# GpSimd forms a sixth of each long part of the weights and finishes the rows in a graph-attention kernel's second stage

## The chip, the cores and the metric

One core of a Trainium2 chip. The metric is the time of one execution on the device, in microseconds. The engines are called as the profile calls them: PE (TensorE), DVE (VectorE), ACT (ScalarE), POOL (GpSimd) and SP (SyncE, which issues DMAs here).

## What is computed

x is [4096, 128] in f32, adj a [4096, 4096] matrix of zeros and ones (about 16 ones in a row), W [128, 128], a [256, 1]. Two layers, cut to their core:

```python
# first layer: for each node the maximum over its neighbours, then a layer norm
out = where(has_nbr, max over neighbours of x, 0)
x = layernorm(x + out)
# second layer: attention over the neighbours
h = x @ W
e = leaky_relu((h @ a_src)[:, None] + (h @ a_dst)[None, :], negative_slope=0.2)
att = softmax(where(valid, e, -1e9), axis=1)            # valid: adj > 0 and h.sum(1) != 0
attention = where(att >= 1e-4, att, 0) * L[:, None]     # L: number of valid neighbours
x = layernorm(x + elu(h + attention @ h))
```

## The kernel before, in words

The 32 tiles of 128 rows are worked on in 8 groups of 4 tiles, the 4096 sources in 32 segments of 128. Each engine has a queue of its own, written out by hand, and the engines meet at semaphores.

**First stage** (to about 620 us). For each group PE turns the adjacency (L1017), ACT writes it out as fp8, and PE, ACT and DVE select the first neighbour of each segment and keep maxima (L1447, one input in PSUM, one in SBUF). POOL clears the gather buffer G (memsets, L687 and L692) and issues the indirect DMAs for further neighbours (L699, L708). These go on for the last groups until about 708 us, beside the start of the second stage. Behind them POOL has nothing to do until `ex_listed`, near the end.

**Second stage.** The attention weights of a group (512 rows) against a segment are one tile [128 sources, 512 rows]. With rho a row factor and r_col a column factor, a weight is (1 + max(rho * r - 1, 0)) * adjacency. `PARTS` cuts the 32 segments into four long parts of 6 segments and two of 4. `ORDER` lists the 48 parts of all groups; from position 23 on the groups 4 to 7 follow nearly one after the other: (4, 0..2) are 23 to 25, (3, 5) is 26, (4, 3..5) 27 to 29, group 5 is 30 to 35, group 6 is 36 to 41, group 7 is 42 to 47. `BEGUN` is 4. For step i of the queues:

- ACT, `relu_part(i)` and `relu_segs` (L843 to L870): one activation of 128x512 for each segment, max(r * rho - 1, 0), into `wbuf[i % 4]`. It waits until PE has used the buffer (`w_used`, four parts earlier). ACT also has exp, log and square root of the finished groups (L906 to L914), each with a table load.
- DVE, `mask_piece(i, n)` (L1688): (w + 1) * adjacency, one instruction for a part from step 14 on (in pieces of two segments ahead of it). It reads two SBUF tensors, and it waits for the loaded adjacency and for `relu_ready`.
- PE, `weigh(i)` (L1217): 4 f32 matmuls a segment, sums in PSUM.

`ENDS` gives the step at which DVE takes the finished sums of each group (23, 26, 29, 32, 35, 38, 43, 49), and `NORM` the step of its last work on it (27, 30, 33, 36, 39, 42, 47, 52). On DVE a group g goes through: `take_sums` at ENDS[g] (L1753): small instructions, four that form u from PSUM (L1773), then e4 = min(u, 0) and p4 = max(u, 0); ACT then takes exp of e4 (`uexp`). `elu_norm` at ENDS[g] + 1 (L1797): y4 = e4 - 1 + p4 (L1802), y4 += x1in (L1805, after which SP may load x1in again, `x1_used`), statistics (L1808, L1811), variance. `find_suspects` follows (L1784). At NORM[g] come `finish` (L1815): reciprocal (L1817) and four instructions of 128x128 that write out4 (L1822), then `place_suspects` (L1826 to L1841), on whose last instruction PE waits in `list_suspects` (L1255, at its step ENDS[g] + 3). For group 7 all this stands at the end, behind the last part. SP stores a group's rows at its step ENDS[g] + 7.

The tail behind 898 us (group 7's rows, then up to 128 suspect rows computed again exactly, then a flag) follows PE's last part.

## Time and profile before

| | |
|---|---|
| runs (3) | 943.18, 944.92, 947.7 us, median 944.92 |
| profiled execution | 951.18 us |
| its span, first to last instruction | 949.4 us |
| busy of the span: PE, DVE, ACT, POOL | 725.3, 586.1, 585.2, 329.9 us |
| mean granted clock of TensorE | 0.847 |

The runs agree within half a per cent. The profiled execution is one more, 0.7% above their median; every duration here comes from it. "Busy" of PE is modelled, so a busy PE is not one at its peak; spans on POOL are rough. In a view of instructions in order of time a row has start, duration, engine, line, operation, out<-in with shapes, and a count of merged instructions; instructions of DVE overlap by some 0.08 us where nothing is waited for, so that start to start is what counts. In square brackets stands the idle time ahead of a row and who ended it.

### The profile page before, as it was taken

The page shows a single profiled execution, that of the slowest core. Times are in us where ns is not written, and L with a number is a line of the kernel's source. Part 1 is how long each engine was busy: PE and PEld are TensorE (multiplying, and loading weights), DVE is VectorE, ACT ScalarE, POOL GpSimd, SP SyncE. Part 2 cuts the span into 40 slices and gives each one's busy share as a digit, 9 for nine tenths or more (in the row PEclk, how much of TensorE's full clock was granted, in tenths as well). Part 3 has the DMA queues.
Part 4 walks back from the last instruction along what each step waited for, and adds up shares of the span by engine and source line. Part 5 has one row for each costly group of instructions (what it writes and reads, how often), then busy time and mean ns, then how long its engine had stood idle before and what let it go on. Part 6 is the DMA issues. An engine that isn't in the chain of part 4 may idle for free.

```text
span 949.4 us, 17279 instructions
## 1 busy us (share of the span) xinstructions
PE 725.3 (76%) x6605; PEld 529.3 (56%) x6675; DVE 586.1 (62%) x1319; ACT 585.2 (62%) x861; POOL 329.9 (35%) x310
## 2 busy tenths in 40 slices
PE   4999469659677946955966783688999798999843
PEld 2566236325334523632633441387999698999832
DVE  4668129337525724833752662499957699999673
ACT  5998248328425724822842653578785799999570
POOL 4101751761462374176157136406860000000020
PEclk9999669668957957976986795789999999999957
DMA  9977436444364434744536121222413123232030
GB/s 187 210 152 157 76 73 134 96 90 103 85 123 88 110 72 82 156 85 88 101 94 129 40 71 27 89 77 80 123 38 101 56 87 87 73 109 59 12 59 2
DMA packets 60512, 87.37 MB, mean 92 GB/s; under 512 B 7714, under 2 KB 33326, under 8 KB 60428
## 3 DMA queue, kind: packets, MB, share of 16 engines
q0 software_dynamic: 27328, 42.14, 26.2%
q1 hardware_dynamic: 33100, 44.10, 14.8%
q8 instruction: 55, 0.90, 0.4%
q14 instruction: 29, 0.24, 0.1%
HBM read 108.12 MB, written 21.04 MB: 136 GB/s over the span
## 4 chain that ended last, share of the span: by engine, by line
PE 35%; DVE 19%; another core or an unknown queue 19%; ACT 10%; issue 10%; POOL 5%; DMA 0%; POOLq 0%; DVEq 0%; ACTq 0%
PE psS L1046 13%; PE psA L1017 5%; PE psR L1027 5%; PE psR L1236 3%; DVE x_split L1694 3%; POOL G L699 3%; DVE acc L1447 3%; DVE adj_in L1694 3%; ACT hot L784 2%; ACT at_home L777 2%; PE psC L1061 2%; PE psC L1065 2%; ACT adj_in L865 1%; ACT x_split L865 1%
## 5 line engine op out<-in xcount | busy, mean ns | idle before, releaser
L1447 DVE TENSOR_TENSOR acc<-acc,psS 128x1024 f32<-128x1024 f32 x120 | 146.2, 1218 | 246.9 <-remote 161.2
L1046 PE MATMUL psS<-hot,x_split 128*128 128x512 bf16 x698 | 217.5, 418 | 51.3 <-issue 41.3
L784 ACT ACTIVATE hot<-psR,is_none 128x512 bf16<-128x512 f32 x256 | 168.6, 703 | 105.4 <-remote 71.9
L699 POOL DMA_INDIRECT G<-in_x_dram,idx x160 | 178.1, 1113 | 124.8 <-DVE idx L1537 78.5
L777 ACT ACTIVATE at_home<-psA 128x1024 fp8e4<-128x1024 bf16 x128 | 133.3, 1041 | 125.1 <-remote 89.9
L1046 PEld LDWEIGHTS psS<-hot,x_split 128*128 128x128 bf16 x768 | 77.3, 103 | 127.4 <-issue 65.9
L1017 PE MATMUL psA<-ident_bf,adj_in 128*128 128x128 bf16 x1024 | 93.5, 234 | 58.7 <-issue 31.4
L1027 PE MATMUL psR<-at_home,first 128*128 128x512 fp8e4 x256 | 106.4, 416 | 12.3 <-issue 8.7
L1017 PEld LDWEIGHTS psA<-ident_bf,adj_in 128*128 128x128 bf16 x1024 | 67.5, 104 | 73.8 <-issue 45.1
L1061 PEld LDWEIGHTS psC<-taken_book,hot 128*128 128x128 bf16 x1024 | 64.1, 100 | 75.9 <-issue 29.8
L708 POOL DMA_INDIRECT G<-in_x_dram,idx_extra x80 | 84.4, 1055 | 39.7 <-issue 22.6
L1694 DVE SCALAR_TENSOR_TENSOR x_split<-x_split,at_home 128x1024 f32<-128x1024 f32 (+2 forms) x36 | 72.7, 2049 | 11.9 <-ACT x_split L865 11.8
L1065 PE MATMUL psC<-codebook,at_home 128*128 128x13 bf16 x1024 | 65.0, 169 | 15.0 <-issue 15.0
L643 POOL DMA_DIRECT2D adj_in<-in_adj_dram x28 | 22.2, 794 | 152.7 <-PE psA L1017 135.7
L1694 DVE SCALAR_TENSOR_TENSOR adj_in<-adj_in,at_home 128x1024 f32<-128x1024 f32 (+2 forms) x40 | 73.2, 1860 | 1.9 <-ACT adj_in L865 1.9
L730 POOL DMA_INDIRECT adj_in<-in_adj_dram,exact_idx x4 | 3.9, 966 | 200.2 <-DVE exact_idx L1936 199.3
L1061 PE MATMUL psC<-taken_book,hot 128*128 128x13 bf16 x1024 | 66.7, 171 | 6.5 <-issue 6.1
L1236 PE MATMUL psR<-at_home,adj_in 128*128 128x130 f32 x416 | 50.4, 283 | 11.3 <-DVE adj_in L1694 11.3
L1236 PEld LDWEIGHTS psR<-at_home,adj_in 128*128 128x128 f32 x416 | 49.3, 198 | 12.5 <-issue 12.5
L865 ACT ACTIVATE x_split<-acc,minus,r_col 128x512 f32<-128x512 f32 x72 | 51.9, 801 | 6.0 <-PE psC L1236 6.0
L1065 PEld LDWEIGHTS psC<-codebook,at_home 128*128 128x128 fp8e4 x1024 | 45.4, 97 | 15.9 <-issue 15.9
L865 ACT ACTIVATE adj_in<-rho,minus,r_col 128x512 f32<-128x512 f32 x72 | 52.2, 803 | 3.3 <-PE psC L1236 3.2
(321 smaller groups left out, 1242.4 us busy)
## 6 DMA issues: line engine op xcount, KB each, us to landing
adj_in<-in_adj_dram POOLq DMA_DIRECT2D x28, 1024.0 KB, 10.8
adjT_dram<-at_home SPq DMA_DIRECT2D x32, 512.0 KB, 7.6
at_home<-adjT_dram SPq DMA_DIRECT2D x32, 384.0 KB
adj_in<-in_adj_dram POOLq DMA_DIRECT2D x8, 512.0 KB, 8.5
at_home<-adjT_dram SPq DMA_DIRECT2D x16, 256.0 KB
G<-in_x_dram,idx POOLq DMA_INDIRECT x160
own<-in_x_dram SPq DMA_DIRECT2D x8, 256.0 KB
x_dram<-x1w SPq DMA_DIRECT2D x8, 256.0 KB
```

The costliest lines, as they stand in the source:

```text
L699: pool.indirect_dma_start(out=G[:, k * GT + t, :], out_offset=None, in_=x, in_offset=bass.IndirectOffsetOnAxis(ap=idx[:, t, k:k + 1], axis=0),
L777: nc.scalar.copy(at[:, 2 * u:2 * u + 2, :], turn_home, saturate=True).then_inc(at_ready, 1)
L784: nc.scalar.activation(hot[:, n % 4, :], psR[:, n % 2, :], ACT.Relu, bias=is_none[:, :]).then_inc(hot_ready, 1)
L865: nc.scalar.activation(home[:, s - s0, :], rho[g % 4], ACT.Relu, bias=minus1[:, :], scale=r_col[:, s:s + 1]).then_inc(relu_ready, 1)
L1017: mm = nc.tensor.transpose(turn_home[:, i, t * P:(t + 1) * P], adj_in[:, k, t, at_col:at_col + SEG], ident_bf[:, :])
L1027: nc.tensor.matmul(psR[:, n % 2, :], first[:, :], at[:, n % SEGS, :], start=True, stop=True).then_inc(ranked, 1)
L1046: mm = nc.tensor.matmul(psS[:, b, s % 2 * ROWS:(s % 2 + 1) * ROWS], x_split[:, k, s, :], hot[:, n % 4, :], start=(k == 0), stop=(k == 2))
L1061: mm = nc.tensor.matmul(code_home[:, t, j, :], hot[:, n % 4, t * P:(t + 1) * P], taken_book[:, :], start=False, stop=False, skip_group_che ...
L1065: mm = nc.tensor.matmul(code_home[:, t, j, :], at[:, s, t * P:(t + 1) * P], codebook[:, :], start=False, stop=True, skip_group_check=True)
L1236: mm = nc.tensor.matmul(sums_of(g, t)[:, 0:D + 2], home[:, s - s0, t * P:(t + 1) * P], h_f[:, s, :], start=(s == 0 and starts(g, t)), stop ...
L1447: V.tensor_tensor(acc_flat, acc_flat, psS[:, b, :], ALU.max).then_inc(free[b], 1)
L1694: mask = V.scalar_tensor_tensor(out=home[:, s0:s1, :], in0=home[:, s0:s1, :], scalar=1.0, in1=ring[:, s0:s1, :], op0=ALU.add, op1=ALU.mult)
```

## The change

POOL gets two jobs in the second stage.

1. For each long part of groups 4 to 7 (16 parts, `BY_POOL`), POOL forms the sixth segment: max(r * rho, 1), which is the relu with its 1 already added, and DVE multiplies that segment by the adjacency in an instruction of its own. ACT forms five segments, and DVE's mask covers five.
2. For groups 0 to 6, POOL does the two additions of `elu_norm` (`add_up`, two instructions of 128x512) and the four instructions that write the rows (`normalised`, 128x128 each). p4 gets its -1 in the instruction that forms it. DVE keeps statistics, variance and reciprocal; its `elu_norm` stands one step later (ENDS[g] + 2). Group 7 is finished on DVE as before.

POOL's queue of this stage stands behind the gathers: step by step relu_one, then normalised at NORM[g] + 1, then add_up at ENDS[g] + 2.

```diff
+BY_POOL = [1 if g >= BEGUN and PARTS[k][1] - PARTS[k][0] == PART else 0 for g, k in ORDER]
+POOL_DONE = [sum(BY_POOL[:i + 1]) for i in range(len(ORDER))]
+RELUS_DONE = [done - by_pool for done, by_pool in zip(SEGS_DONE, POOL_DONE)]
...
+            def add_up(g):
+                if g:
+                    pool.wait_ge(out_ready, g)
+                pool.wait_ge(uexp_ready, g + 1)
+                pool.wait_ge(pos_ready, g + 1)
+                nc.gpsimd.tensor_tensor(y4, e4, p4, ALU.add).then_inc(pool_step, 1)
+                pool.wait_ge(pool_step, g + 1)
+                pool.wait_ge(x1_loaded[g % 2], 16 * (g // 2 + 1))
+                nc.gpsimd.tensor_tensor(y4, y4, x1in[:, g % 2, :, :], ALU.add).then_inc(x1_used, 1)
+
+            def normalised(g):
+                pool.wait_ge(rstd_ready, g + 1)
+                if g >= 2:
+                    pool.wait_ge(out_stored[g % 2], 16 * (g // 2))
+                for t in range(GT):
+                    last = nc.gpsimd.tensor_scalar(out4[:, g % 2, t, :], y4[:, t, :], mv[:, t, 0:1], rstd[:, t:t + 1],
+                                                   ALU.subtract, ALU.mult)
+                last.then_inc(out_ready, 1)
+
+
+            def relu_one(i):
+                g, k = ORDER[i]
+                pool.wait_ge(w_used, i - WEIGHTS_AHEAD + 1)
+                pool.wait_ge(rho_ready, g - BEGUN + 1)
+                nc.gpsimd.tensor_scalar(wbuf[i % WEIGHTS_AHEAD][:, PART - 1, :], rho[g % 4],
+                                        r_col[:, PARTS[k][1] - 1:PARTS[k][1]], 1.0, ALU.mult, ALU.max
+                                        ).then_inc(pool_relu_ready, 1)
+
+            for i in range(len(ORDER) + STEPS_AFTER):
+                if i < len(ORDER) and BY_POOL[i]:
+                    relu_one(i)
+                for g in range(GROUPS - 1):
+                    if i == NORM[g] + 1:
+                        normalised(g)
+                    if i == ENDS[g] + 2:
+                        add_up(g)
...
             def relu_part(i):
                 s0, s1 = PARTS[ORDER[i][1]]
-                relu_segs(i, 0, s1 - s0)
+                relu_segs(i, 0, s1 - s0 - BY_POOL[i])
...
-                dve.wait_ge(relu_ready, (SEGS_DONE[i - 1] if i else 0) + s1)
+                dve.wait_ge(relu_ready, (RELUS_DONE[i - 1] if i else 0) + s1)
                 mask = V.scalar_tensor_tensor(out=home[:, s0:s1, :], in0=home[:, s0:s1, :], scalar=1.0, in1=ring[:, s0:s1, :],
                                               op0=ALU.add, op1=ALU.mult)
+                if BY_POOL[i]:
+                    dve.wait_ge(pool_relu_ready, POOL_DONE[i])
+                    mask = V.tensor_tensor(home[:, s1:PART, :], home[:, s1:PART, :], ring[:, s1:PART, :], ALU.mult)
...
-                V.tensor_scalar(p4, u4, 0.0, None, ALU.max).then_inc(dve_step, 1)
-                own_t.n += 1
-                return own_t.n
-
-            pos_mark = {}
+                V.tensor_scalar(p4, u4, 0.0, -1.0, ALU.max, ALU.add).then_inc(pos_ready, 1)
...
             def elu_norm(g):
-                after(pos_mark[g])
+
+                if g == GROUPS - 1:
+                    dve.wait_ge(out_ready, g)
+                    dve.wait_ge(uexp_ready, g + 1)
+                    dve.wait_ge(pos_ready, g + 1)
+                    a = mark(V.tensor_tensor(y4, e4, p4, ALU.add))
+                    after(a)
+                    dve.wait_ge(x1_loaded[g % 2], 16 * (g // 2 + 1))
+                    V.tensor_tensor(y4, y4, x1in[:, g % 2, :, :], ALU.add).then_inc(x1_used, 1)
+                dve.wait_ge(x1_used, g + 1)
                 if g:
                     dve.wait_ge(out_ready, g)
-                dve.wait_ge(uexp_ready, g + 1)
-                a = mark(V.scalar_tensor_tensor(out=y4, in0=e4, scalar=-1.0, in1=p4, op0=ALU.add, op1=ALU.add))
-                after(a)
-                dve.wait_ge(x1_loaded[g % 2], 16 * (g // 2 + 1))
-                V.tensor_tensor(y4, y4, x1in[:, g % 2, :, :], ALU.add).then_inc(x1_used, 1)
-                dve.wait_ge(x1_used, g + 1)
...
             def finish(g):
                 dve.wait_ge(std1_ready, g + 1)
+                if g < GROUPS - 1:
+                    V.reciprocal(rstd[:, :], std[:, :]).then_inc(rstd_ready, 1)
+                    return
...
+                            elu_norm(g)
+                        else:
+                            find_suspects(g)
+                    if i == ENDS[g] + 2 and g < GROUPS - 1:
                         elu_norm(g)
-                        if g < GROUPS - 1:
-                            find_suspects(g)
                     if i == ENDS[g]:
-                        pos_mark[g] = take_sums(g)
+                        take_sums(g)
```

## Rows read from the trace of the kernel before

**Rows 1.** Windows: stretch, its length, busy us (and instructions) by engine, PEclk, DMA share, GB/s
```profile
757.00:812.00 55.00, 50.95 (x435) 49.63 (x436) 53.45 (x124) 53.14 (x71) 0.00 (x0) 0.97 0.28 80
812.00:867.00 55.00, 51.28 (x445) 50.36 (x443) 51.88 (x125) 54.46 (x74) 0.00 (x0) 0.97 0.31 93
867.00:898.00 31.00, 30.83 (x277) 30.62 (x277) 23.07 (x46) 18.47 (x25) 0.00 (x0) 1.00 0.11 30
```

**Rows 2.** Waits of 757 to 898 us: total, times, longest
```profile
PE psS L1259 <- DVE base L1841: 6.2, 3, 2.8
...
PE psR L1236 <- DVE G L1773: 3.5, 1, 3.5
...
DVE x_split L1694 <- ACT x_split L865: 2.8, 2, 1.6
```

**Rows 3.** Timeline of DVE: sums of group 2 and of group 4
```profile
788.79 1.13 DVE L1773 SCALAR_TENSOR_TENSOR G<-psS,h_seg 128x128 f32<-128x128 f32 x4
...
824.56 1.13 DVE L1773 SCALAR_TENSOR_TENSOR G<-psR,h_seg 128x128 f32<-128x128 f32 x4
```

**Rows 4.** Timeline of PE: the wait for group 5's suspects
```profile
866.94 1.16 PE L1259 MATMUL psS<-h_seg,C 128*128 128x134 f32 x8 [0.87 <-DVE base L1841]
```

**Rows 5.** Timeline of DVE, masks and finishing work between 845 and 855 us
```profile
845.26 3.35 DVE L1694 SCALAR_TENSOR_TENSOR x_split<-x_split,at_home 128x3072 f32<-128x3072 f32 x1
...
848.73 1.12 DVE L1822 TENSOR_SCALAR G<-G,mv,rstd 128x128 f32<-128x128 f32 x4
849.76 0.22 DVE L1830 TENSOR_SCALAR sus_at<-psS,base 128x4 f32<-128x4 f32 x1
...
850.42 0.69 DVE L1838 TENSOR_TENSOR C<-place_iota,sus_at 128x512 f32<-128x512 f32 x1
851.03 0.15 DVE L1841 TENSOR_TENSOR base<-base,psS 128x1 f32<-128x1 f32 x1
851.09 0.68 DVE L1802 SCALAR_TENSOR_TENSOR G<-G 128x512 f32<-128x512 f32 x1
...
852.54 0.87 DVE L1808 BATCH_NORM_STATS2 stats<-G 128x6 f32<-128x128 f32 x4
...
854.60 2.29 DVE L1694 SCALAR_TENSOR_TENSOR adj_in<-adj_in,at_home 128x2048 f32<-128x2048 f32 x1
```

**Rows 6.** Timeline of ACT: six relus of a long part
```profile
864.90 4.33 ACT L865 ACTIVATE adj_in<-acc,minus,r_col 128x512 f32<-128x512 f32 x6
```

**Rows 7.** Groups by form on POOL: count, busy us, mean ns, idle before
```profile
L687 POOL MEMSET G<- 128x2560 f32 x8 | 17.9, 2242 | 45.6 <-DVE gmax L1579 45.6
L692 POOL MEMSET G<- 128x1280 f32 x8 | 9.5, 1188 | 0.0
...
L667 POOL IOTA seg<- 128x320 f32 x1 | 1.2, 1170 | 0.0
```

**Rows 8.** One line's instructions (ns, least/median/greatest), and the timelines of DVE and POOL
```profile
L1492 DVE CAST key_int<-level x8: 188/191/2322, 85.2 to 637.4; 128x64 int32<-128x64 f32 x8
...
637.40 2.32 DVE L1492 CAST key_int<-level 128x64 int32<-128x64 f32 x1
...
637.44 2.23 POOL L687 MEMSET G<- 128x2560 f32 x1 [22.91 <-DVE gmax L1579]
...
L1447 DVE TENSOR_TENSOR acc<-acc,psS x120: 1202/1221/1223, 26.0 to 615.7; 128x1024 f32<-128x1024 f32 x120
```

**Rows 9.** Groups to 640 us and of 640 to 710 us; timelines of POOL and DVE
```profile
L699 POOL DMA_INDIRECT G<-in_x_dram,idx x140 | 141.4, 1010 | 111.1 <-DVE idx L1537 70.7 <-issue 40.5
...
L699 POOL DMA_INDIRECT G<-in_x_dram,idx x20 | 36.8, 1838 | 13.6 <-DVE idx L1537 7.9 <-issue 5.8
...
682.94 7.13 POOL L699 DMA_INDIRECT G<-in_x_dram,idx  x1 [0.30 <-issue]
...
699.78 3.36 DVE L1694 SCALAR_TENSOR_TENSOR x_split<-x_split,at_home 128x3072 f32<-128x3072 f32 x1 [1.51 <-ACT x_split L865]
...
700.92 3.10 POOL L708 DMA_INDIRECT G<-in_x_dram,idx_extra  x1 [0.30 <-issue]
```

More of the change, by code:

```diff
@@ L396, in build @@
         relu_ready = sem("relu_ready")
+        pool_relu_ready = sem("pool_relu_ready")
         w_ready = sem("w_ready")
@@ L428, in build @@
         neg_ready = sem("neg_ready")
+        pos_ready = sem("pos_ready")
+        pool_step = sem("pool_step")
+        rstd_ready = sem("rstd_ready")
         ex_neg_ready = sem("ex_neg_ready")
@@ L838, in spread_rho @@
                     act.wait_ge(s_spread, g - BEGUN + 1)
-                    act.wait_ge(relu_ready, SEGS_DONE[AT[g - 4, NPARTS - 1]])
+                    act.wait_ge(relu_ready, RELUS_DONE[AT[g - 4, NPARTS - 1]])
+                    if POOL_DONE[AT[g - 4, NPARTS - 1]]:
+                        act.wait_ge(pool_relu_ready, POOL_DONE[AT[g - 4, NPARTS - 1]])
                     from_ps, done = psS[:, 0, 0:ROWS], rho_ready
@@ L1683, in pieces @@
                 g, k = ORDER[i]
-                m = PARTS[k][1] - PARTS[k][0]
+                m = PARTS[k][1] - PARTS[k][0] - BY_POOL[i]
                 step = 2 if i < BY_PIECES else m
@@ L1997, in _ @@
             dve.wait_ge(ex_u_ready, 1)
+            dve.wait_ge(out_ready, GROUPS)
             V.tensor_scalar(e4[:, 0, :], u4[:, 0, :], 0.0, None, ALU.min).then_inc(ex_neg_ready, 1)
```

## The prediction

> **What bounds the kernel now.** The windows view comes first, because an average over the span mixes stages: from 757 us, when the first group of rows is taken, to 867 us, PE, DVE and ACT are all busy for over nine tenths of the time and POOL not at all [rows 1]. So any of the three could be the limit, and the waits decide. In that stretch PE waits for DVE: 3.5 us once at its head, where it waits for group 0 to be taken, and 6.2 us in three waits for the last instruction of place_suspects; DVE waits for ACT 2.8 us in two waits [rows 2]. DVE is the limit by a little. Its period shows it too: from group 2's sums to group 4's is 35.8 us for two groups, with DVE going from instruction to instruction [rows 3]. Behind 867 us it turns: the last wait of PE for DVE ends at 866.9 us, with 0.87 us [rows 4], and from there PE is busy for 30.8 of 31 us at full clock [rows 1]. So **the end of the stage is the time of place_suspects of group 5 (DVE's step 42) plus 31 us of PE work**, and behind that comes a tail that the change leaves alone but for group 7's own rows, which stay on DVE. A microsecond taken from or given to DVE ahead of step 42 counts fully; one behind it doesn't, as DVE is busy for only 23 of those 31 us [rows 1]. POOL's last work of before is the gathering, over before the stretch starts, so the cover for what POOL gets is an idle engine, and the question is what that engine shares with DVE.
>
> **What is taken away.** Ahead of step 42 six groups (0 to 5) are finished. In each DVE loses the two additions, from 851.09 to 852.54, 1.45 us, and the four instructions that write the rows, 848.73 to 849.76, 1.03 us [rows 5]. That is 2.48 us a group, 14.9 us in all. Adding -1 in the instruction that forms p4 costs nothing: it is a second scalar operation in the same pass. ACT loses one relu of each long part of groups 4 to 7. Six of them take 4.33 us with the first at 0.80, so 0.71 each [rows 6]; 13 lie at or before step 42, 9.2 us. That alone moves nothing, since ACT is not the last to arrive, but it keeps ACT from becoming the bound when DVE is relieved: ACT is idle for only 2.4 of 110 us [rows 1].
>
> **What is added on DVE.** The mask of a long part is two instructions. One of 3072 elements takes 3.35 us and one of 2048 takes 2.29 [rows 5], 0.53 us a segment; the segment that splits off costs what a 128x512 instruction with two inputs costs from start to start, 850.42 to 851.03, 0.61 us [rows 5]. So 0.08 us each, 13 times, 1.0 us. DVE's net own saving is 13.9 us. SP's queue keeps its instructions; stores of a group wait for out_ready, which now comes about a step later, and go out 7 steps behind the group's end, so they still fit.
>
> **What is added on POOL, and its price.** 13 relus ahead of step 42, and for each of six groups two additions of 128x512 and four instructions of 128x128. No elementwise instruction that reads SBUF runs on POOL in this trace, so I bound it. Below: memsets of 2560 and 1280 elements take 2.24 and 1.19 us, 0.82 ns an element and 0.14 us on top [rows 7], so 0.56 us for 512 elements and 0.25 for 128. Above: an iota of 320 elements takes 1.17 us [rows 7], 3.7 ns an element, 1.87 us for 512. A relu has one input and one output and lies near the memset: 0.6 us. An addition brings two inputs, and I take twice the input time: 1.0 us. The four of 128 elements take 0.28 each. A group is then 2.0 + 1.1 = 3.1 us, six are 18.7, 13 relus 7.8, together **26.5 us of POOL** (20.0 with the low prices; some 58 with the iota's, which I don't believe for a plain stream). The Trainium skill (GPSIMD Engine Reference, section 3.1) gives 4497 ns for a tensor_tensor of 2048 elements, so by it an addition is an estimated 1.1 us and the sum below would be 1 us more; no run here shows it.
>
> **What POOL's time does to DVE.** This decides. At 637.40 us DVE starts a CAST of 64 elements that takes 0.19 us seven times of eight; this once it takes 2.32 us and ends when a memset on POOL ends that began 0.04 us later [rows 8]. DVE stood still for a whole POOL instruction. The other way round, a gather's issue on POOL takes 1.01 us on average up to 640 us, where DVE works mostly from PSUM, and 1.84 us behind it, where the masks run [rows 9]; the one at 700.92 us takes 3.10 us because a mask runs until 703.14, and one sat through six masks, 7.13 us [rows 9]. Against this stands stage one's maximum, whose one input is in PSUM: 120 of them lie between 1202 and 1223 ns, memsets beside some of them [rows 8]. So the two engines share something that masks and SBUF-to-SBUF scalar instructions need, and that is held for whole instructions. What no row shows is a POOL instruction that reads hundreds of elements against a mask: the bounds are none of POOL's time charged to DVE and all of it. DVE's instructions that do without are mainly the four with sums from PSUM, 1.13 us [rows 3], and the statistics, 0.87 us [rows 5], with small ones some 3 us of the 15.5 a group that DVE has left. That speaks for 0.8; POOL's instructions that fall into these run free, and I take 0.75. POOL then costs DVE 19.9 us, and the sum at step 42 is -14.9 + 1.0 + 19.9 = **+6.0 us**, carried to the end. The profiled execution, 951.2 us (span 949.4), becomes 957.2; it lies 6.3 us above the median of the runs, 944.9, which I take as base: **950.9 us**. With low prices and a share of 0.6 the sum is -2; with relus at 0.8, additions at 1.3 and a share of 0.8, +12.
>
> The Trainium skill (SBUF — State Buffer, Who interferes with whom) says just this: a DVE instruction with two SBUF inputs contends with a GpSimd one that reads SBUF, a 2-port one with any, and whoever is second blocks for the whole instruction. By it the share is near 1 and the sum +13; by a reading in which only POOL waits, it is the second rival. The trace agrees for the CAST (2.32 us) and for POOL's side; for a mask behind a reading POOL instruction no run here shows it.
>
> **Rivals.** (1) *POOL never holds a mask.* For it: every mask of 1024 elements beside POOL's issues keeps its price, and only a CAST was seen held. Then DVE saves 13.9 us, but PE can't use it all: its waits of 6.2 us and the low clock of 812 to 867 us (0.97 over 55 us, 1.65 us lost) are all that goes [rows 1, 2, 4], 7.9 us. Then 937.0 us, and PE bounds. It decides once less than 0.52 of POOL's time (13.9 of 26.5) falls on DVE; this is the other side. (2) *The exchange comes out even*, share 0.4 to 0.55: within 4 us of 945. (3) *POOL comes late.* DVE's step for the statistics waits for x1_used, hence for six POOL instructions in a row that each may sit behind a mask. DVE idles there, so that POOL's time counts in full: 26.5 less 13.9, +13 us, 958 us. Queued behind that wait are the masks, and PE behind them. For it: the 7.13 us [rows 9]; against: a whole mask and place_suspects lie between rstd_ready and the wait, 5 us. That the change doesn't do what it says is excluded by the wait structure: DVE can't mask a last segment without pool_relu_ready.
>
> **Chances.** A measurement of this kernel tells about 0.5% from no change, 4.7 us. The forecast case, -2 to +12 with its middle at +6, has 0.50; rival 1 has 0.25, rival 2 0.10, rival 3 0.15. Slower by over 0.5%: 0.31 of the forecast case and 0.14 of rival 3, 0.45. Within: 0.16 + 0.03 of rival 1 + 0.08 + 0.01, 0.28. Faster: the rest, 0.27. Both signs are well filled, so the range takes in rival 1 and most of the rest: 936 to 958; the likeliest case alone is 943 to 957.
>
> **What would show it.** Masks of 2560 elements at 2.82 us in their shortest, with many at 3.4 or more and ends that agree with ends of POOL instructions; 512-element masks between 0.7 and 1.4; POOL relus of 0.6 us at best and of several us where they sit behind a mask; periods of two groups at 37 to 38 us, not 35.8; PE's waits for L1841's successor longer than 6.2 us, with more time at the low clock; place_suspects of group 5 ending near 873 us; PE without a wait behind it. Masks all at 2.82 and 0.69 and a period near 32 us would be rival 1; long waits of DVE for x1_used, rival 3. I am wrong in kind if DVE's time per group falls.

## The result, and the profile after

The change makes the kernel slower by 1%: 953.43 us (950.57 to 958.69, 4 runs) against 944.25 us (943.18 to 947.7, 4 runs) for the kernel before on the same chip, **ratio 1.0095 with a 95% interval of 1.0069 to 1.0121**. The forecast was 950.9 us on a base of 944.9, +6.0; measured is +9.2. Sign, size and range held, and the mechanism behind them mostly did not.

The profiled execution of after takes 950.57 us (span 948.7), less than the 951.18 of before: the start of the second stage moves by some microseconds from execution to execution (the first sums of group 0 come at 749.44 us here, at 756.91 in the trace of before), and the tail takes 49.0 or 50.6 us. So the traces are compared by the stretch that the prediction was about, from the first sums of group 0 to the start of the last instruction of place_suspects of group 5 (step 42). It took 109.73 us before and takes **118.09 us** after, +8.4; from there to the sums of group 7 it is 32.16 us in both.

Section 1 of after's page:

```profile
PE 725.0 (76%) x6605; PEld 530.4 (56%) x6675; DVE 578.7 (61%) x1293; ACT 573.7 (60%) x845; POOL 439.6 (46%) x368
```

The windows of after, columns as in [rows 1]:

```profile
757.00:812.00 55.00, 49.12 (x421) 47.92 (x420) 47.64 (x118) 46.47 (x61) 32.45 (x19) 0.97 0.24 74
812.00:867.00 55.00, 48.53 (x408) 47.46 (x406) 41.40 (x96) 45.54 (x63) 41.34 (x24) 0.94 0.28 89
867.00:898.00 31.00, 30.18 (x273) 30.19 (x274) 23.95 (x44) 18.28 (x24) 20.74 (x12) 1.00 0.12 35
```

POOL gains 110 us over the whole span and DVE loses 7. But in the second window DVE is busy for 41.4 us where it was for 51.9 [rows 1], ACT for 45.5 instead of 54.5 and PE for 48.5 instead of 51.3: **no engine is full any more**. Over the stretch DVE is busy for 97 of 118 us, where it was for 105 of 110. A stage in which all have slack and all are slower is bound by a chain through several of them. The waits of after, 757 to 900 us, name its links:

```profile
POOL G L751 <- DVE rstd L1868: 43.0, 7, 12.5
ACT std L962 <- DVE mv L1863: 17.8, 7, 3.5
...
PE psS L1307 <- DVE base L1894: 12.8, 5, 4.2
DVE stats L1858 <- POOL G L744: 11.8, 5, 3.1
...
DVE adj_in L1742 <- ACT adj_in L913: 4.7, 4, 1.8
DVE x_split L1742 <- ACT x_split L913: 4.3, 4, 1.7
```

DVE waits for POOL (11.8 us), ACT for DVE's variance (17.8, a wait that before doesn't have in this window), and DVE for ACT's relus. PE's wait for place_suspects is 12.8 us where it was 6.2 [rows 2]. One turn of the chain, group 4, in the timelines of DVE, POOL and ACT:

```profile
828.59 0.17 DVE L1868 RECIPROCAL rstd<-std 128x4 f32<-128x4 f32 x1
...
828.86 6.14 POOL L751 TENSOR_SCALAR G<-G,mv,rstd 128x128 f32<-128x128 f32 x4 [4.87 <-DVE rstd L1868]
...
830.99 2.83 DVE L1742 SCALAR_TENSOR_TENSOR adj_in<-adj_in,at_home 128x2560 f32<-128x2560 f32 x1 [0.21 <-ACT adj_in L913]
...
835.09 1.27 POOL L741 TENSOR_TENSOR G<-G 128x512 f32<-128x512 f32 x1
836.44 1.27 POOL L744 TENSOR_TENSOR G<-G 128x512 f32<-128x512 f32 x1
...
837.74 0.87 DVE L1858 BATCH_NORM_STATS2 stats<-G 128x6 f32<-128x128 f32 x4 [3.11 <-POOL G L744]
...
839.26 0.20 ACT L962 ACTIVATE std<-mv 128x4 f32<-128x4 f32 x1 [3.55 <-DVE mv L1863]
839.37 3.62 ACT L913 ACTIVATE x_split<-acc,minus,r_col 128x512 f32<-128x512 f32 x5
```

rstd comes at 828.8; POOL writes group 3's rows in 6.1 us (they free y4) and adds group 4's up by 837.7, 8.9 us in all. DVE has a mask and small work for 5.8 of them and stands for the other 3.1. ACT has stood since 835.7 before its square root, and its next five relus, which wait for nothing else, start only behind it. DVE's groups by form in the stretch (columns as in [rows 7]):

```profile
L1742 DVE SCALAR_TENSOR_TENSOR x_split<-x_split,at_home 128x2560 f32<-128x2560 f32 x7 | 19.8, 2822 | 1.9 <-ACT x_split L913 1.9
L1742 DVE SCALAR_TENSOR_TENSOR adj_in<-adj_in,at_home 128x2560 f32<-128x2560 f32 x6 | 16.9, 2822 | 0.2 <-ACT adj_in L913 0.2
L1742 DVE SCALAR_TENSOR_TENSOR adj_in<-adj_in,at_home 128x2048 f32<-128x2048 f32 x4 | 10.1, 2523 | 3.3 <-ACT adj_in L913 3.3
...
L1746 DVE TENSOR_TENSOR adj_in<-adj_in,at_home 128x512 f32<-128x512 f32 x6 | 5.2, 863 | 0.0
...
L1807 DVE TENSOR_SCALAR lnrho<-h_seg,cols 128x4 f32<-128x4 f32 x5 | 2.7, 537 | 0.0
```

The masks of 2560 elements keep 2.82 us without exception: 13 of them, and POOL is at work for 74 of the 110 us from 757 to 867. POOL is mostly the one held: a line's own instructions (ns, least, median, greatest) show what the same one takes free and beside masks.

```profile
L760 POOL TENSOR_SCALAR x_split<-rho,r_col x4: 1997/2000/3616, 741.2 to 781.4; 128x512 f32<-128x512 f32 x4
L741 POOL TENSOR_TENSOR G<-G x7: 1267/1273/3360, 751.9 to 879.3; 128x512 f32<-128x512 f32 x7
L751 POOL TENSOR_SCALAR G<-G,mv,rstd x28: 789/802/3700, 771.4 to 894.6; 128x128 f32<-128x128 f32 x28
```

But a mask can be held too. One of 2048 elements, which had waited for ACT, begins 0.2 us behind an addition of POOL and takes 3.22 us for 2.29; the second addition then sits under it (timelines of DVE and POOL):

```profile
775.05 3.22 DVE L1742 SCALAR_TENSOR_TENSOR adj_in<-adj_in,at_home 128x2048 f32<-128x2048 f32 x1 [1.77 <-ACT adj_in L913]
...
774.85 1.27 POOL L741 TENSOR_TENSOR G<-G 128x512 f32<-128x512 f32 x1
776.20 3.20 POOL L744 TENSOR_TENSOR G<-G 128x512 f32<-128x512 f32 x1
```

### The profile page after: what moved, and what is told of

The parts are those of the page before. It is cut to its first block, busy times and chain, and to the rows that moved or that the text cites. A ratio compares the mean times of both kernels' runs of the same rounds, so it can differ in the third digit from the quotient of the medians.

```text
span 948.7 us, 17319 instructions
## 1 busy us (share of the span) xinstructions
PE 725.0 (76%) x6605; PEld 530.4 (56%) x6675; DVE 578.7 (61%) x1293; ACT 573.7 (60%) x845; POOL 439.6 (46%) x368
## 3 DMA queue, kind: packets, MB, share of 16 engines
q1 hardware_dynamic: 33100, 44.10, 14.4%
## 4 chain that ended last, share of the span: by engine, by line
PE 36%; another core or an unknown queue 18%; issue 13%; POOL 11%; DVE 11%; ACT 9%; DMA 0%; POOLq 0%; ACTq 0%; DVEq 0%
PE psS L1094 14%; PE psA L1065 5%; PE psR L1075 4%; PE psR L1284 3%; POOL G L707 3%; DVE acc L1495 3%; POOL G L751 2%; ACT hot L830 2%; ACT at_home L823 2%; PE psC L1109 2%; PE psC L1113 2%; POOL x_split L760 2%; POOL G L741 1%; POOL adj_in L760 1%
## 5 line engine op out<-in xcount | busy, mean ns | idle before, releaser
L716 POOL DMA_INDIRECT G<-in_x_dram,idx_extra x80 | 86.6, 1082 | 39.1 <-issue 22.6
L1742 DVE SCALAR_TENSOR_TENSOR x_split<-x_split,at_home 128x1024 f32<-128x1024 f32 (+3 forms) x36 | 68.5, 1933 | 12.6 <-ACT x_split L913 12.6
L1742 DVE SCALAR_TENSOR_TENSOR adj_in<-adj_in,at_home 128x1024 f32<-128x1024 f32 (+2 forms) x40 | 70.5, 1791 | 6.6 <-ACT adj_in L913 6.6
L913 ACT ACTIVATE x_split<-acc,minus,r_col 128x512 f32<-128x512 f32 x68 | 49.0, 800 | 6.0 <-PE psC L1284 6.0
L751 POOL TENSOR_SCALAR G<-G,mv,rstd 128x128 f32<-128x128 f32 x28 | 32.0, 1154 | 43.0 <-DVE rstd L1868 43.0
L913 ACT ACTIVATE adj_in<-rho,minus,r_col 128x512 f32<-128x512 f32 x68 | 49.3, 801 | 3.3 <-PE psC L1284 3.2
## 6 DMA issues: line engine op xcount, KB each, us to landing
adj_in<-in_adj_dram POOLq DMA_DIRECT2D x28, 1024.0 KB, 10.5
```

Source lines behind the costliest of these rows:

```text
L913: nc.scalar.activation(home[:, s - s0, :], rho[g % 4], ACT.Relu, bias=minus1[:, :], scale=r_col[:, s:s + 1]).then_inc(relu_ready, 1)
L1742: mask = V.scalar_tensor_tensor(out=home[:, s0:s1, :], in0=home[:, s0:s1, :], scalar=1.0, in1=ring[:, s0:s1, :], op0=ALU.add, op1=ALU.mult)
```

## Theories and the yardstick

The 8.4 us can be put together from after's own trace: -14.9 + 1.0 of DVE's work, 11.8 of waiting for POOL, 5.3 more of waiting for ACT (6.9 in the stretch, 1.6 before), and 5.2 by which DVE's own instructions grew (each form's mean over its mean before, times its count). That is +8.4, but a sum doesn't say what would go away with what. Three theories: **held**, the forecast's, that POOL's instructions stop DVE's; **late**, rival 3, that DVE waits for POOL's result; and **order**, which the prediction didn't have: `elu_norm` stands a step later, so ACT, whose square root keeps its place at NORM - 1, stands in front of its relus.

Two runs measure the yardstick. The kernel before takes 762 to 763 us on three of the chips used and 944 to 945 on two, so every ratio is to before on the same chip.

before_again, no edit:

> The kernel before once more, as a measure of the yardstick itself. The experiments' stretches, from the first sums of group 0 to the last instruction of place_suspects of group 5, are all set against the one trace of before, which has 109.7 us, and some of them ran on a chip whose whole time is 762 us and not 945. If the stretch is a property of the kernel alone, this run has 109.7 us within 1 us and periods of two groups at 35.6 to 35.8 us, whatever its whole time, and the ratio is 1.000 within 0.3%. If the stretch differs by 2 us or more on another chip, then the differences of 3 us and less between experiments (relus_only, norm_only, norm_relus) can't be read from it, and only the ratios stand.

Measured: 762.71 us, ratio 1.0008 [0.9980, 1.0036]; stretch 109.70 us and the same periods, with the whole run 188 us shorter: the first sums come at 570.5 us for 756.9, and the mean granted clock is 0.956 for 0.847. So the stretch belongs to the kernel and not to the chip, within 0.1 us.

after_again, no edit to after:

> The changed kernel once more, as the control for the others of this chip. All theories: 8 to 10 us above the kernel before, the stretch from the first taking of sums to place_suspects of group 5 at 118 us against 110.

Measured: 954.29 against 945.08 us, 1.0109 [1.0081, 1.0136]; stretch 118.14 us. The result repeats, and together with before_again it makes a tenth of a microsecond in the stretch readable, and 3 us in a ratio.

All stretches and ratios together (DVE's waits in the stretch, us):

| kernel | stretch, us | against before | DVE waits for POOL | for ACT | ratio to before [95%] |
|---|---|---|---|---|---|
| before | 109.7 | | 0 | 1.6 | 1 |
| after | 118.1 | +8.4 | 11.8 | 6.9 | 1.0095 [1.0069, 1.0121] |
| beside | 120.2 | +10.5 | 0 | 0 | 1.0162 [1.0093, 1.0231] |
| beside_memset | 124.1 | +14.4 | 0 | 0.5 | 1.0183 [1.0153, 1.0213] |
| relus_only | 112.8 | +3.1 | 0 | 0.5 | 1.0064 [1.0035, 1.0093] |
| rows_only | 116.7 | +7.0 | 4.8 | 12.8 | 1.0167 [1.0105, 1.0228] |
| late_sqrt | 117.1 | +7.4 | 13.2 | 4.9 | 1.0131 [1.0069, 1.0194] |
| stats_later | 117.7 | +8.0 | 0 | 9.3 | 1.0126 [1.0085, 1.0166] |
| add_first | 110.1 | +0.3 | 0 | 1.7 | 1.0009 [0.9984, 1.0034] |
| norm_only | 108.4 | -1.4 | 0 | 6.3 | 1.0004 [0.9983, 1.0025] |
| norm_relus | 107.4 | -2.3 | 0 | 1.6 | 0.9972 [0.9945, 0.9998] |
| norm_half | 105.0 | -4.8 | 0 | 1.6 | **0.9925 [0.9898, 0.9951]** |

## How much does POOL hold DVE?

**beside.** The kernel before, with after's POOL work done on a tile nobody reads; it starts where after's would, and nobody waits for it.

```diff
+            for i in range(len(ORDER) + STEPS_AFTER):
+                if i < len(ORDER) and ORDER[i][0] >= BEGUN and ORDER[i][1] < 4:
+                    pool.wait_ge(w_used, i - WEIGHTS_AHEAD + 1)
+                    beside(side[:, 1, :], side[:, 0, :], 1.0, 1.0, ALU.mult, ALU.max, op=nc.gpsimd.tensor_scalar)
+                for g in range(GROUPS - 1):
+                    if i == NORM[g] + 1:
+                        pool.wait_ge(std1_ready, g + 1)
+                        for t in range(GT):
+                            beside(side[:, 1, t * P:(t + 1) * P], side[:, 0, t * P:(t + 1) * P], 1.0, 1.0, ALU.mult, ALU.max,
+                                   op=nc.gpsimd.tensor_scalar)
+                    if i == ENDS[g] + 2:
+                        pool.wait_ge(uexp_ready, g + 1)
+                        for k in range(2):
+                            beside(side[:, 1, :], side[:, 0, :], side[:, 0, :], ALU.add, op=nc.gpsimd.tensor_tensor)
```

> The kernel before, with POOL doing instructions of the change's kinds and sizes at the same steps on a scratch tile of its own that nobody reads (16 scalar instructions of 128x512, and for each of seven groups two additions of 128x512 and four scalar instructions of 128x128). Nobody waits for POOL; the only way to lose time is that DVE is held. Held theory (my forecast, with the prices now seen: 2.0, 1.27 and 0.80 us, 60 us of POOL ahead of DVE's step 42, three quarters on DVE): 985 us or more. POOL-late theory (POOL sits behind masks, a mask never sits behind POOL, only small scalar instructions do): 944 to 948 us.

Measured: +10.5 us of stretch, 774.69 us against 762.60. That is neither of the two expectations, and lies nearer the second. DVE's groups by form in the stretch:

```profile
L1719 DVE SCALAR_TENSOR_TENSOR adj_in<-adj_in,at_home 128x3072 f32<-128x3072 f32 x6 | 20.1, 3352 | 0.0
L1847 DVE TENSOR_SCALAR G<-G,mv,rstd 128x128 f32<-128x128 f32 x24 | 11.3, 545 | 0.2
...
L1827 DVE SCALAR_TENSOR_TENSOR G<-G 128x512 f32<-128x512 f32 x6 | 6.0, 995 | 0.0
```

The row instructions go from 344 to 545 ns (4.8 us in all), the additions and the comparison that places the suspects (L1863) grow by a third each, and the masks keep 3.35 but for one, which takes 3.76. All growth is 12.5 us, against some 60 us that POOL's instructions would take unheld (13 x 2.0 + 12 x 1.27 + 24 x 0.80 = 60.4, with the least times above; this run's own are a little shorter, 1.92, 1.04 and 0.64): a share of 0.2. Which instructions are hit depends on what stands ahead of them:

```profile
630.20 3.35 DVE L1719 SCALAR_TENSOR_TENSOR adj_in<-adj_in,at_home 128x3072 f32<-128x3072 f32 x1
...
633.67 2.49 DVE L1847 TENSOR_SCALAR G<-G,mv,rstd 128x128 f32<-128x128 f32 x4
...
630.79 4.77 POOL L734 TENSOR_TENSOR side<-side 128x512 f32<-128x512 f32 x2 [1.48 <-ACT G L935]
```

POOL's additions arrive at 630.79 under a mask and come through only behind it, where they stop the four row instructions, 2.49 us for 1.12.

**beside_memset.** The same with POOL only writing: memsets of 2048, 1344 and 768 elements in the places of relus, additions and row instructions.

```diff
-                    beside(side[:, 1, :], side[:, 0, :], 1.0, 1.0, ALU.mult, ALU.max, op=nc.gpsimd.tensor_scalar)
+                    beside(side[:, 0:4, :], 1.0, op=nc.gpsimd.memset)
...
-                            beside(side[:, 1, t * P:(t + 1) * P], side[:, 0, t * P:(t + 1) * P], 1.0, 1.0, ALU.mult, ALU.max,
-                                   op=nc.gpsimd.tensor_scalar)
+                            beside(side[:, 0:2, 0:384], 1.0, op=nc.gpsimd.memset)
...
-                            beside(side[:, 1, :], side[:, 0, :], side[:, 0, :], ALU.add, op=nc.gpsimd.tensor_tensor)
+                            beside(side[:, 0:3, 0:448], 1.0, op=nc.gpsimd.memset)
```

> The side run once more with memsets of about the same lengths (2048, 1344 and 768 elements: 1.8, 1.2 and 0.8 us) in place of the instructions that read, so that POOL only writes. If what is held is the second read of SBUF, masks and two-input instructions pass and the stretch is 110 to 113 us (scalar instructions from SBUF to SBUF may still be held, as the CAST was); POOL's memsets keep their own length beside masks. If any POOL instruction holds and is held alike: 120 us as in the side run.

Measured: +14.4 us, more than either expectation had. The line of the row instructions (ns, least, median, greatest):

```profile
L1846 DVE TENSOR_SCALAR G<-G,mv,rstd x32: 329/346/1984, 774.7 to 919.1; 128x128 f32<-128x128 f32 x32
```

One turn in DVE's timeline:

```profile
832.09 3.34 DVE L1718 SCALAR_TENSOR_TENSOR adj_in<-adj_in,at_home 128x3072 f32<-128x3072 f32 x1
...
835.56 3.58 DVE L1846 TENSOR_SCALAR G<-G,mv,rstd 128x128 f32<-128x128 f32 x4
```

The long memsets as a group in the stretch:

```profile
L734 POOL MEMSET side<- 128x2048 f32 x13 | 23.6, 1818 | 30.4 <-PE psC L1260 10.7 <-PE psS L1260 9.6 <-PE psR L1260 9.5
```

And POOL's timeline beside that turn of DVE's:

```profile
832.65 6.34 POOL L734 MEMSET side<- 128x1344 f32 x4 [1.09 <-ACT G L934]
```

A memset runs beside a mask and neither notices: 1.82 us for 2048 elements, which is [rows 7]'s 0.82 ns an element and 0.14 us, and no mask over 3.36 us. The additions and L1862, with two inputs in SBUF, keep 0.69 us as well. What is stopped are scalar instructions from SBUF to SBUF: the row instructions in three of the six groups, and small ones of 4 elements. Durations count such a stop twice, since the instruction queued behind the stopped one has begun too; from start to start the row instructions lose 6.4 us and the small ones most of the other 9. So there are two pairings: **a POOL instruction that reads gets in the way of a two-input DVE one and the other way round; scalar SBUF-to-SBUF ones on DVE are stopped by a POOL instruction that only writes as well.** The Trainium skill (SBUF — State Buffer, Who interferes with whom) has just these two cases, and both runs agree with it. It also says that whoever issues first goes first and the other blocks for the whole instruction. The addition and the 2048-element mask of after, above, agree. A relu of POOL doesn't: in relus_only one of 1.99 us begins 0.12 us ahead of a mask at 578.33 us, and the mask takes 3.25 us for 2.82, so that the two run side by side for most of the relu. How often each engine comes second, which decided the price here, has to be read from the trace.

## The parts of the change

**relus_only.** POOL's relus and the split masks alone; groups are finished on DVE at their old step.

```diff
-            def add_up(g):
...
-            def normalised(g):
...
-            for i in range(len(ORDER) + STEPS_AFTER):
-                if i < len(ORDER) and BY_POOL[i]:
+            for i in range(len(ORDER)):
+                if BY_POOL[i]:
                     relu_one(i)
```

> The kernel before with the sixth segment of the 16 long parts on POOL, rows finished on DVE as before. Held theory: 13 relus of 2.0 us ahead of step 42, three quarters on DVE, and 1 us for the split masks: 965 us. POOL-late theory: a relu on POOL (2 us, with a mask ahead of it 4.7) fits beside five on ACT (3.6 us) or is late by about 1 us; DVE stays the bound and its own work grows by 0.08 us a part: 945 to 949 us.

Measured: +3.1 us, ratio 1.0064 [1.0035, 1.0093], as the second expectation had it. The split masks cost 1.0, DVE's instructions grow by 3.4, and 1.1 of waiting for ACT goes, +3.3 together. DVE is the bound here and ACT isn't, so relieving ACT alone buys only that wait.

**rows_only.** After with `BY_POOL` all 0: additions and rows on POOL, all relus on ACT.

```diff
-BY_POOL = [1 if g >= BEGUN and PARTS[k][1] - PARTS[k][0] == PART else 0 for g, k in ORDER]
+BY_POOL = [0 for g, k in ORDER]
```

> The change without the relus on POOL: additions and row-writing of groups 0 to 6 on POOL, statistics a step later. Held theory: 34 us of POOL for six groups, three quarters on DVE, less 14.9: 955 us. POOL-late theory: the chain from the reciprocal over six POOL instructions to the statistics stays, so most of the loss stays: 948 to 954 us. If the relus make the chain late, it is gone without them and the kernel is below before: 938 to 942 us.

Measured: +7.0 us, ratio 1.0167 [1.0105, 1.0228]; the loss stays, and is not gone without the relus. By its trace -14.9 + 5.7 of growth + 4.8 for POOL + 11.2 more for ACT = +6.8. Without relus in its queue POOL is less late (4.8 for 11.8). But ACT has all its relus again and still stands 8.4 us for the variance, and DVE waits for it nearly twice as long (12.8 for 6.9). Of 19 masks five are held here, by 0.17 to 1.09 us, each behind a wait of DVE for ACT in which POOL's additions began. The two parts sum to +10.1, more than the change's 8.4: it seems that POOL's relus give ACT back part of what the later step takes from it.

## Late, or order?

**late_sqrt.** After with ACT's square root of groups 0 to 6 one step later, to match.

```diff
-                    if i == NORM[g] - 1:
+                    if i == NORM[g] - (g == GROUPS - 1):
```

> The change with ACT's square root of groups 0 to 6 one step later in ACT's queue (NORM[g] in place of NORM[g] - 1), behind the relus of that step. Theory that ACT's standing still for the variance (17.8 us in all against none before) is what delays the relus: DVE's 9.0 us of waits for ACT fall to about 3 and the time falls by 4 to 6 us, to 947 to 949 us. Theory that the chain over POOL bounds the period whatever ACT does: within 2 us of the change, 951 to 955 us.

Measured: +7.4 us, 1 us better than after by the stretch; the ratio, 1.0131 [1.0069, 1.0194], can't tell it from after. ACT's wait for the variance is gone and stands at its next instruction instead (waits of late_sqrt, in the stretch):

```profile
ACT G L958 <- DVE G L1828: 18.2, 6, 4.6
DVE stats L1858 <- POOL G L744: 13.2, 5, 3.1
```

Its next instruction is the exponential, which waits for DVE's sums. DVE is the one that is behind, and moving ACT's place in the queue doesn't bring it forward. The same move in stats_later, where POOL is idle, was not run.

**stats_later.** The kernel before with nothing but the order changed: `elu_norm` one step later, all of it on DVE, POOL idle.

```diff
                     if i == ENDS[g] + 1:
...
-                        elu_norm(g)
-                        if g < GROUPS - 1:
+                            elu_norm(g)
+                        else:
                             find_suspects(g)
+                    if i == ENDS[g] + 2 and g < GROUPS - 1:
+                        elu_norm(g)
```

> The kernel before with nothing on POOL and only the change's order on DVE: additions and statistics of groups 0 to 6 one step later. Theory that the later step alone makes ACT stand still for the variance and the relus late: 3 to 5 us slower, stretch 113 to 115 us. Theory that this order costs nothing unless POOL is late: the stretch stays at 110 us within 1, the kernel within 2 us of before.

Measured: **+8.0 us, ratio 1.0126 [1.0085, 1.0166], as much as the whole change**, with not one instruction moved to another engine, and more than the 3 to 5 us expected. Its waits in the stretch:

```profile
PE psS L1259 <- DVE base L1841: 10.5, 4, 4.4
ACT std L914 <- DVE mv L1813: 8.3, 6, 2.2
DVE adj_in L1694 <- ACT adj_in L865: 5.4, 4, 2.4
DVE x_split L1694 <- ACT x_split L865: 3.9, 3, 2.4
```

And one turn in ACT's timeline:

```profile
631.27 5.74 ACT L865 ACTIVATE x_split<-rho,minus,r_col 128x512 f32<-128x512 f32 x8
637.02 1.28 ACT L914 ACT_TABLE_LOAD   x1
639.67 0.21 ACT L914 ACTIVATE std<-mv 128x4 f32<-128x4 f32 x1 [1.36 <-DVE mv L1813]
639.78 4.33 ACT L865 ACTIVATE adj_in<-acc,minus,r_col 128x512 f32<-128x512 f32 x6
```

ACT stands 8.3 us in six waits, and DVE's wait for ACT grows from 1.6 to 9.3, 7.7 us, which is the loss. ACT was busy for 53.1 and 54.5 of 55 us [rows 1], so a microsecond in which it stands for DVE comes back to DVE as a late relu.

**add_first.** After with y4, mv and rstd doubled, so that POOL adds group g + 1 up ahead of writing group g's rows. DVE's statistics no longer stand behind six POOL instructions; the later step stays.

```diff
+        y4s = [y4, y[:, :, :]]
+        mvs, rstds = [mv, sb("mv_odd", [P, GT, 2])], [rstd, sb("rstd_odd", [P, GT])]
...
-                if g:
-                    pool.wait_ge(out_ready, g)
+                if g > 1:
+                    pool.wait_ge(out_ready, g - 1)
...
-                    if i == NORM[g] + 1:
-                        normalised(g)
                     if i == ENDS[g] + 2:
                         add_up(g)
+                for g in range(GROUPS - 1):
+                    if i == NORM[g] + 1:
+                        normalised(g)
```

> The change with y4, mean and reciprocal held twice (groups take turns), so that POOL can do the additions of group g + 1 ahead of writing the rows of group g; POOL's amount of work is the same. Theory that the chain rstd, six POOL instructions, statistics costs the time: DVE's 11.8 us of waits for POOL fall below 3 and the stretch falls from 118 to 107 to 111 us, the kernel to 2 us below or at the kernel before. Theory that it is the amount of POOL's work that holds DVE: no change against the change, 118 us.

Measured: +0.3 us, ratio 1.0009 [0.9984, 1.0034]; DVE waits for nobody but 1.7 us for ACT. Taking rival 3's wait out gains 8.0 us. The expectation that blamed the chain holds, though 11.8 us of waits gone bring only 8.0. By the difference, DVE's instructions now grow by 14.1 us (-13.9 + 0.1 + 14.1 = +0.3), nearly three times after's 5.2. DVE's groups in the stretch show where:

```profile
L1749 DVE TENSOR_TENSOR adj_in<-adj_in,at_home 128x512 f32<-128x512 f32 x6 | 7.3, 1222 | 0.0
...
L1890 DVE SCALAR_TENSOR_TENSOR sus_at<-sus_at,suspect 128x4 f32<-128x4 f32 x6 | 4.8, 794 | 0.2
```

The twelve split masks take 1.22 us for 0.685 (6.4 us in all) and L1890, four elements wide, 0.79 for 0.16. While DVE stood waiting, POOL ran free; now that it doesn't stand, the two meet. Part of what looked like a wait for a result was time that POOL needs from DVE in either form. That fits stats_later too: the later step cost 8.0 us there, presumably because ACT was full, and here, with 12 relus fewer on ACT, DVE's wait for it is down to 1.7.

## What can be kept

**norm_only.** After with `BY_POOL` all 0, y4, mv and rstd doubled as in add_first, and both additions and `elu_norm` back on DVE at ENDS + 1. POOL only writes the rows, and nobody on the path waits for them.

```diff
-                    if i == ENDS[g] + 2:
-                        add_up(g)
...
+                            elu_norm(g)
                         else:
                             find_suspects(g)
-                    if i == ENDS[g] + 2 and g < GROUPS - 1:
-                        elu_norm(g)
```

> Only the row-writing of groups 0 to 6 on POOL (with y4, mean and reciprocal held twice), additions back on DVE at their old step, no relus on POOL. DVE saves 6.2 us ahead of step 42 and nobody waits for POOL. If POOL holds DVE as in the side run (a fifth of its 19 us, about 4 us), the stretch is 107 to 109 us and the kernel 1 to 3 us faster than before. Held theory with three quarters: 8 us slower.

Measured: -1.4 us of stretch, as expected, but ratio 1.0004 [0.9983, 1.0025], where 1 to 3 us less were expected; behind the stretch it loses 1.7 us again (below). DVE is relieved of six times 1.03 us, its instructions grow by only 0.3, and 4.7 of the 6.2 come back as waits for ACT (6.3 for 1.6): ACT is now the bound.

**norm_relus** and **norm_half.** norm_only with POOL's relus for all 16 long parts, or for 8 (the first and the fourth of each group).

```diff
-BY_POOL = [0 for g, k in ORDER]
+BY_POOL = [1 if g >= BEGUN and k in (0, 3) else 0 for g, k in ORDER]
```

> norm_only with all 16 sixth segments on POOL, which is the change without its two additions and with the doubled buffers. POOL has about 13 x 2.0 + 24 x 0.8 = 45 us of work in 110 us. Cheap-POOL theory: ACT relieved by 9.2 us, DVE -6.2 + 1.0 + 3.4 of holds as in relus_only: stretch 107 to 108.5 us, the kernel 1 to 3 us below before. Theory that the relus wait behind the row-writing (3.2 us and masks): DVE waits for them and the stretch is 110 us or more.

> norm_only with the sixth segment of 8 of the 16 long parts (the first and the fourth of each group) on POOL as well. In norm_only ACT had become the bound: DVE waited 12.2 us for it ahead of step 42. Theory that POOL's work is cheap as long as nobody waits for a chain over it: ACT is relieved by 0.71 us in each of 7 parts ahead of step 42, DVE gets 0.6 us of splits and about 1.5 us of holds; the stretch falls from 108.3 to 105 to 107 us and the kernel to 2 to 5 us below before. Theory that any relu on POOL costs as in relus_only (3 us for 13): 110 us, no gain.

Measured: norm_relus -2.3 us and 0.9972 [0.9945, 0.9998]; norm_half **-4.8 us and 0.9925 [0.9898, 0.9951]**, 756.62 against 763.15 us, the clear gain of the two. It beats the kernel before and, by the stretch, after by 13.1 us. Its windows and its waits in the stretch:

```profile
568.00:620.00 52.00, 48.66 (x415) 47.31 (x415) 50.56 (x122) 49.82 (x67) 14.04 (x11) 0.97 0.29 84
620.00:673.00 53.00, 51.62 (x464) 50.78 (x463) 50.01 (x111) 52.05 (x71) 18.72 (x16) 1.00 0.31 93
```

```profile
PE psS L1307 <- DVE base L1893: 2.7, 2, 2.1
...
DVE x_split L1742 <- ACT x_split L913: 1.6, 1, 1.6
```

PE, DVE and ACT are all full again, PE's clock is at 1.00 in the second window, and PE's wait for place_suspects is half of before's in the same stretch (2.7 us for 5.3). Eight relus free ACT enough that its wait stays at 1.6; sixteen buy no more of that and the stretch is 2.5 us longer. Other choices of eight parts were not run, so number and place of the relus are not told apart.

## Why the prediction was right, and where it wasn't

- **What bounds the stage**: held in the main. The time of DVE's step 42 sets the end; the 32.16 us behind it stayed. That a microsecond taken from DVE "counts fully" did not hold: norm_only takes 6.2 us and the stretch falls by 1.4, as ACT then bounds. Three variants (norm_only, rows_only, stats_later) have 1.4 to 1.7 us more behind step 42, and that is PE's clock, a mean of 0.95 in each: in norm_only it is 0.74 from 859 to 864 us, where a wait of 2.3 us for step 42 ends, and 1.00 from 870 us on. Its window, where before has the clock at 1.00 [rows 1]:

```profile
859.00:894.00 35.00, 32.54 (x277) 32.36 (x277) 24.20 (x53) 21.17 (x30) 9.61 (x8) 0.95 0.11 31
```

  The same 277 matmuls take 32.5 us there and 30.8 in before [rows 1]. Whether a kernel meets this is a second small term that the sum didn't have.
- **DVE's own saving, 14.9 less 1.0**: held by the accounts of after, rows_only and norm_only (six times 1.03 less 4.7 less 0.3 is 1.2, measured 1.4).
- **POOL's prices**: wrong. A relu takes 2.0 us and not 0.6, a 128-wide row instruction 0.80 and not 0.28, an addition 1.27 and not 1.0. The total is 60 us and not 26.5: the bound from the iota, 58, which "I don't believe for a plain stream", was the right one. The memset I went by moves a write-only stream at 0.82 ns an element; the instruction with one input and two scalar operations takes 3.9, and that with two inputs 2.5. Of the addition, the Trainium skill (GPSIMD Engine Reference, section 3.1) had the better estimate, 1.1 us, against the 1.27 measured.
- **The share of 0.75**: wrong the other way. 5.2 of 60 us in after is 0.09, in beside 0.2, and 14.1 in add_first still only 0.23. The reading "held for whole instructions" was right of additions and wrong of relus, and wrong of who waits: POOL mostly waits under the masks, and few masks are stopped (none of 2560 elements in after). The product, 19.9 us, is 14.7 more than the 5.2 by which DVE's instructions grew. Against that the sum had no term for waits, and DVE waits 17.1 us more than before, 11.8 for POOL and 5.3 for ACT. **So the number was good by luck: a term 14.7 us too large stood in for one of 17.1 us that was missing.** By the Trainium skill's rule (SBUF — State Buffer, Who interferes with whom), read as a share near 1, the sum was to be +13; with POOL's true prices that reading would give +46, and no run comes near it. The reading in which only POOL waits, which the prediction calls the second rival, is its rival 1.
- **Rival 3**: the nearest to what happened. DVE waits 11.8 us in five waits for L744, with the cover of about 5 us that the prediction named (5.8 in the turn shown), and add_first shows it worth 8.0 us. Its price, +13, came from the same wrong terms and was too high. I gave it 0.15 because the POOL work to be covered was 3.1 us a group by my prices; with 8.9 it could not have been hidden, so the wrong price also set the wrong chance.
- **The missed step**: of the step that is moved I followed DVE's queue, SP's and POOL's, and not ACT's. `elu_norm` a step later makes the variance late; ACT's square root kept its place, at ENDS + 3, with the relus of the next parts queued behind it. stats_later alone costs +8.0. The sentence "ACT is not the last to arrive" was true of before, and this edit made it false.
- **Rival 1**, POOL never holds a mask: its premise is true of the masks of 2560 elements in after, though not of one of 2048, and its conclusion doesn't follow. DVE is held at small instructions and split masks, and waits. norm_half comes nearest to rival 1, with nobody waiting for the rows on POOL: -4.8 us.
- **Signs**: periods of two groups of 39.0 us (predicted 37 to 38), PE's waits longer (12.8) with a lower clock (0.94 for 0.97 in the second window), both as said; place_suspects of group 5 at 867.5 and not near 873 is because the whole stage began 7.5 us earlier. No mask of 2560 elements took 3.4 us, and no relu 0.6. The mark for being wrong in kind, DVE's time per group falling, did appear if busy time is meant (97.2 us in the stretch for 105.2), and so did long waits for x1_used.

What stays open: how the 8.4 us divide between late and order. Each alone is worth about 8 us (add_first takes the one out of after, stats_later puts the other into before), and they don't add; that is as if both made the same chain longer, which no run shows by itself. Nor was it tried to have after's additions on POOL with the statistics at the old step.

## What to carry to other kernels

An engine taken as idle help should get work that nobody waits for: the same rows on POOL shortened the stretch by 1.4 us once their buffers were doubled and the statistics stayed at their step, and lengthened it when POOL stood in the middle of the chain from DVE over ACT to DVE. When a step is moved in one in-order queue, follow every queue that waits for its result and ask what stands behind that wait; here that alone cost as much as the whole change. And when ACT and DVE are both full, relieve both: here rows alone gained nothing (ratio 1.0004), relus alone lost, and rows with half the relus gained 0.75%.

## What the runs showed of the hardware that I had not expected

- POOL's elementwise prices in f32: one input and two scalar operations 2.0 us for 128x512 and 0.80 for 128x128; two inputs 1.27 for 128x512. The instruction with fewer inputs is the slower one.
- Masks are seldom held: 13 of 2560 elements at 2.82 us each in after, beside a POOL busy for two thirds of the time. Most that are held follow a wait or a small instruction of DVE (after, at 775.05 us, 0.93 us longer; rows_only, five of 19), but in beside one directly behind another took 3.76 us for 3.35. More often it is an instruction four elements wide that waits for a POOL one (L1890 in add_first, 0.79 us for 0.16).
- A relu of POOL holds a mask for less than its own length: in relus_only 0.42 us, while the two overlap for 1.87 (at 578.33 us). An addition held the mask of after nearly to its end, 0.93 of 1.07 us.
- Whether POOL reads matters: beside write-only memsets masks and two-input instructions of 512 elements keep their times, and the memsets theirs, but scalar SBUF-to-SBUF ones are stopped (a row instruction up to 1.98 us for 0.34), so that a POOL which reads nothing cost DVE more (+14.4 us) than one that reads and adds (+10.5).
